# Two graph layers over an edge list: 432 tiles of one bucket each become 332 pure and 50 mixed tiles, and the second layer moves into the loop's block

## The reference

```python
def layer0(h, edges, W, b):            # 41,250 edges (src, tgt), 1,250 nodes, 512 features
    x_ij = concatenate([h[src], h[tgt]], axis=1)        # 41,250 x 1,024
    m_ij = relu(x_ij @ W.T + b)                         # W: 512 x 1,024
    return segment_sum(m_ij, src, 1250)

def layer1(h, src, dst, edge_weight, W, alpha):
    g = h @ W.T
    out = segment_sum(g[src] * edge_weight[:, None], dst, 1250)
    return where(out >= 0, out, alpha * out)

h = maximum(layernorm(x), 0);  x = x + layer0(h, ...)
h = maximum(layernorm(x), 0);  x = x + layer1(h, ...)
```

## Time and profile before

| | us |
|---|---|
| median of 3 runs (lowest, highest) | 1081.85 (1081.13, 1082.65) |
| profiled execution | 1083.92 |
| its span | 1082.2 |
| first placing column starts (DVE) | 40.78 |
| first edge product starts | 287.18 |
| last edge product starts | 951.92 |
| W1's load is issued | 961.23 |
| first second-layer product starts | 971.90 |

### The profile page before, as it was taken

The page is one execution under the profiler, slowest core; times in us unless marked ns, Lnnn a source line. Parts: engine busy times, 40 slices in busy tenths (PEclk is TensorE's granted clock), DMA queues, the critical chain, the costliest instruction groups (busy, mean ns, idle before and its releaser), DMA issues. The chain is left out here.

```text
span 1082.2 us, 22605 instructions
## 1 busy us (share of the span) xinstructions
PE 1023.7 (95%) x4879; PEld 814.1 (75%) x4880; DVE 949.4 (88%) x1801; ACT 836.0 (77%) x1769; POOL 716.6 (66%) x1042
## 2 busy tenths in 40 slices
PE   5698999999799999999999999999999999959997
PEld 4386887777588788777888777777778877748775
DVE  7798899888599999999999999999999999973454
ACT  6777798788688888888888888888888888844210
POOL 3888787867567777777777777777777777730000
PEclk9999999999899999999999999999999999979999
DMA  7000000000111111111111111111111111010011
GB/s 209 2 2 3 2 3 2 4 2 2 54 44 43 42 43 39 43 41 41 44 38 43 42 43 43 38 43 42 42 43 38 43 42 42 25 39 1 20 34 42
DMA packets 37249, 38.15 MB, mean 35 GB/s; under 512 B 5990, under 2 KB 33431, under 8 KB 37212
## 3 DMA queue, kind: packets, MB, share of 16 engines
q1 hardware_dynamic: 32512, 37.07, 11.0%
q0 software_dynamic: 4416, 0.30, 1.6%
q10 hardware_dynamic: 284, 0.33, 0.1%
HBM read 34.04 MB, written 3.36 MB: 35 GB/s over the span
## 5 line engine op out<-in xcount | busy, mean ns | idle before, releaser
L1076 ACT ACTIVATE msg_hi<-edge_ps 128x512 fp32r<-128x512 f32 x432 | 257.8, 597 | 81.7 <-PE edge_ps L1000 81.7
L930 POOL TENSOR_TENSOR M<-M,pair_w 125x125 f32 x432 | 210.9, 488 | 162.0 <-DVE pair_w L1134 122.5
L1148 DVE SCALAR_TENSOR_TENSOR msg_lo<-edge_ps,msg_hi 128x512 fp32r<-128x512 f32 x432 | 290.8, 683 | 20.7 <-ACT msg_hi L1076 15.1
L374 POOL DMA_INDIRECT edge_table<-fields,row_no x136 | 176.7, 1299 | 50.3 <-issue 40.5
L914 POOL TENSOR_TENSOR hot_w<-hot_d,weight_l 128x252 fp32r<-128x252 bf16 x216 | 180.8, 837 | 0.0
L737 ACT ACTIVATE lane_piece<-hot_lane,fields 125x128 fp32r<-125x128 bf16 x498 | 155.6, 391 | 30.6 <-DVE hot_lane L455 30.2
L955 PE MATMUL node_ps<-msg_hi,hot_s 128*125 128x512 f32 x432 | 176.5, 409 | 0.2 <-DVE msg_lo L1148 0.2
L994 PE MATMUL edge_ps<-b_hi,turned_d 125*128 x432 | 172.8, 400 | 1.3 <-ACT turned_d L1060 0.7
L624 PE MATMUL psum<-hot_tile,lane_piece 125*128 125x432 f32 x582 | 157.2, 394 | 16.5 <-ACT lane_piece L737 16.3
L999 PE MATMUL edge_ps<-a_hi,turned_s 125*128 x432 | 171.4, 397 | 0.1
L995 PE MATMUL edge_ps<-b_lo,turned_d 125*128 x432 | 171.3, 397 | 0.0
(11 more groups left out here) (206 smaller groups left out, 1726.6 us busy)
## 6 DMA issues: line engine op xcount, KB each, us to landing
spread<-edge_rows SPq DMA_DIRECT2D x214, 125.0 KB
out_dram<-result SPq DMA_DIRECT2D x10, 250.0 KB
edge_table<-fields,row_no POOLq DMA_INDIRECT x136, 2.6
w_in<-in_L_gnn_W_dram SPq DMA_DIRECT2D x1, 2048.0 KB, 11.6
S<-in_x_dram SPq DMA_DIRECT2D x1, 1792.0 KB
w_in<-in_L_gnn_W_dram SPq DMA_DIRECT2D x1, 1024.0 KB, 5.2
S<-in_x_dram SPq DMA_DIRECT2D x1, 448.0 KB
edge_table<-zeros SPq DMA_DIRECT2D x1, 432.0 KB, 15.3
```

What stands on the lines that cost most here:

```text
L374: pool.indirect_dma_start(table_dram[:, :], bass.IndirectOffsetOnAxis(ap=row_no[:, c:c + 1], axis=0), fields[:, c, 0:TABLE_FIELDS], None). ...
L930: pool.tensor_tensor(part, part, pair_w[h][:, j, 0, 0:BN], ALU.add).then_inc(m_added, 1)
L1076: act.activation(msg_hi[j][:], edge_ps[j][:], ACT.Relu).then_inc(hi_ready, 1)
L1148: dve.scalar_tensor_tensor(out=msg_lo[j][:], in0=edge_ps[j][:], scalar=0.0, in1=msg_hi[j][:].bitcast(F32), op0=ALU.max, op1=ALU.subtract). ...
```

## The change

Each bucket used to fill up its last tile alone. Now the buckets of a source block and two neighbouring destination blocks (2p, 2p+1) share one mixed tile. The 50 mixed tiles come first in the tables (52 columns, 13 groups, MIXC = 52) and last in time; the other edges lie in 332 pure tiles (83 groups), which run as before. NT goes from 432 to 384.

- Slots: the tile counts of a bucket pair are rounded so that the rest of both goes to the pair's mixed tile; a third row beside base_hi and base_lo (`base_up`) moves the odd bucket's slots by multiples of 65536 when they pass its pure tiles. `slots` decodes this with 12 instead of 5 steps. An edge's code has a sign for "odd destination block"; decoding gives local_d (negative for odd in mixed tiles) and local_o = -local_d, so that a one-hot of either is empty for the other's edges.
- Counts: the counting products for chunk k+2 stand seven columns before the end of chunk k, and ACT's copy one column before it.
- A mixed tile has six edge products: two for the even, two for the odd destination block (third one-hot `turned_o`, one buffer), two for the source block; addresses are constants. Its weights product is two products of 252 columns (both destination blocks side by side) that sum high and low in PSUM. Odd tiles' weights are copied by ACT and added to M by POOL in one addition of 250 columns, even ones' are added by DVE directly from PSUM.
- node_ps is summed over the five mixed tiles of a source block and added to S once; then DVE makes the block's statistics, beside the following tiles.
- The second layer's programs follow in the same block, without the barrier between blocks. W1's load is issued once the last edge product is through. Each result is stored as 112 and 13 rows.
- hot_d and hot_s are made from a 16-bit iota (`iota_h`), hot_d has room for two destination blocks, `square` is bf16.

```diff
+NBP = NBLK // 2
+NMIX = NBLK * NBP
+MGRP = -(-NMIX // GRP)
+MIXC = MGRP * GRP
+NGRP = -(-(E // TILE + NBLK * (PAIR - 1)) // GRP)
+PURE = NGRP * GRP
+NT = MIXC + PURE
+COUNT_BACK, COPY_BACK = 7, 1
...
                     def slots(k):
+                        quotient, upper, whole, after = (planes[:, i, :] for i in range(4))
+                        tile, at = tile_no[:, k % 2, :], lane[:, k % 2, :]
+                        own(dve.tensor_reduce(slot[:], planes.rearrange("p b c -> p c b"), AX.X, ALU.add))
+                        own(dve.tensor_scalar(quotient, slot[:], -MID_SLOT, 1.0 / UPPER, ALU.add, ALU.mult))
+                        own(dve.tensor_scalar(upper, quotient, MAGIC, -MAGIC, ALU.add, ALU.add))
...
+                            part = i - last + COUNT_BACK
+                            if k + 2 < NCHUNK and 0 <= part < 3:
+                                count(k + 2, range(CHUNK // 3 * part, CHUNK // 3 * (part + 1)))
...
+                            if k + 2 < NCHUNK and i == FIRST[k + 1] - FIRST[k] - 1 - COPY_BACK:
+                                copy_counts(k + 2)
...
+                def weigh_mixed(m):                                       # POOL
+                    u, j = divmod(m, GRP)
+                    h = m % 2
+                    if j == 0:
+                        pool.wait_ge(hots_d, NGRP + u + 1)
+                    if m < 2:
+                        pool.wait_ge(m_ready, NGRP * 2 + h - 1)
+                    else:
+                        pool.wait_ge(mix_ps, m - 1)
+                    for f, part in enumerate((weight_h[:].bitcast(F32), weight_l)):
+                        pool.tensor_tensor(hot_w[h][:, f], hot_d[(NGRP + u) % 2][:, :, j, :],
+                                           part[:, m:m + 1].unsqueeze(2).to_broadcast([P, 2, OHW]), ALU.mult).then_inc(mix_weighed, 1)
+                def add_mixed(m):
+                    pool.wait_ge(mix_copied, (m + 1) // 2)
+                    blocks = M[:, 2 * m:2 * m + 2, :]
+                    pool.tensor_tensor(blocks, blocks, pair_w[1][:, 0, :, 0:BN], ALU.add).then_inc(mix_pooled, 1)
+                for m in range(2, NMIX):
+                    weigh_mixed(m)
+                    if m % 2 == 1 and m > GRP:
+                        add_mixed(m - GRP)
...
+                def edges_mixed(m):                                       # PE
+                    if j == 0:
+                        pe.wait_ge(turned, n + 1)
+                    pe.matmul(ps, turned_d[k][:, at], b_hi[:, first], start=True, stop=False)
+                    pe.matmul(ps, turned_d[k][:, at], b_lo[:, first], start=False, stop=False)
...
+                    if j == 0:
+                        pe.wait_ge(turned, n + 3)
+                    pe.matmul(ps, turned_o[:, at], b_hi[:, second], start=False, stop=False)
+                    pe.matmul(ps, turned_o[:, at], b_lo[:, second], start=False, stop=True).then_inc(edge_ready, 1)
...
+                for m in range(NMIX):
+                    edges_mixed(m)
+                    if m < 2:
+                        sum_tile(NGRP - 1, PAIR + m, (NGRP - 1) % 2)
+                    else:
+                        sum_mixed(m - 2)
+                    if m in (1, 3):
+                        weights(NGRP - 1, (NGRP - 1) % 2, m // 2)
+                    if m >= GRP:
+                        weights_mixed(m - GRP)
...
+                def next_mixed(v, j):                                     # ACT
+                    made = (turned_d[g % 2], turned_s[g % 2], turned_o)
+                    if j > 0:
+                        one_hot_of(n + j, made[j - 1])
+                    if j < 3:
+                        act.wait_ge(turned, n + j)
...
+                        act.activation(square[:], spread[pair + f][:], ACT.Square, bias=minus_no[0:BN, :],
+                                       scale=-1.0 if j == 2 else 1.0).then_inc(squared, 1)
+                def copy_mixed(m):
+                    act.wait_ge(mix_ps, m + 1)
...
+                        act.wait_ge(mix_pooled, m // 2)
+                    act.copy(pair_w[1][:, 0], m_ps[1][:, 0]).then_inc(mix_copied, 1)
...
+                sp.wait_ge(edge_ready, PURE + NMIX)
+                sp.dma_start(w1_in[:], w1.rearrange("(o p) i -> p o i", p=P)).then_inc(w1_loaded, 16)
+                for b in range(NBLK):
+                    sp.wait_ge(out_ready, b + 1)
+                    for rows in SPLIT:
+                        sp.dma_start(out[b * BN:(b + 1) * BN, :][rows], result[b % 2][rows]).then_inc(stored[b % 2], 16)
```

More of the change, by code:

```diff
@@ L101, in build @@
         ident = sb("ident", [P, P], F32)
-        iota = sb("iota", [P, NT], F32)
+        iota_h = sb("iota_h", [P, P], F16)
         ident_b = sb("ident_b", [P, P], BF16)
@@ L1034, in _ @@
                 turn(0, second=True)
[L1035 removed]
+                with pe.Fori(1, TURNS) as it:
                     turn(it)
[L1037 to L1044 removed]
+                at = offsets(REST)
@@ L1424, in build @@
+        tail.close()
         scope_m.close()
```

766 lines of the change are left out of this document (473 added, 293 removed).

## The result

| | before | after |
|---|---|---|
| median of 4 runs each, same chip (us) | 1082.25 (1081.13 to 1084.27) | 1026.09 (1022.98 to 1027.34) |
| profiled execution, its span | 1083.92, 1082.2 | 1027.34, 1025.4 |
| first placing column starts | 40.78 | 48.50 |
| last placing column starts | 274.6 | 278.5 |
| first edge product starts | 287.18 | 290.91 |

The ratio is 0.9475, 95% interval 0.9448 to 0.9502: faster by 5.0 to 5.5%. 1021 was forecast, 1009 to 1037 the range.

The account below looks back on a forecast made before the run. PE was taken to pace the edge loop, with DVE 3% behind. Loop start 284.2, pure tiles 511.5, mixed 108.1, hole 8.4 and second layer 109.0 sum to a span of 1021.2 us; forecast 1021, range 1009 to 1037.

Parts of the forecast that it names:

- the 3 for hand-overs: Mixed tiles: late turned_o and the change from pure to mixed tiles cost 3 us, bounds 0 and 10.
- held by 0.18: Mixed groups: the next turned_o is ready 2.85 us after the tile's start, PE needs it at 3.03.
- Rivals 1 and 4: Mixed tiles: 1, POOL paces them, +29, 1050, chance 0.15; 4, PE waits for turned_o every group, 1106, chance 0.02.
- Rival 2: First part: added steps are paid, stalls only move to another wait; +11.7 instead of -3, 1036, chance 0.13.
- rival 3: First part gains all it can, hand-overs cost nothing: -7 and -3, 1011, chance 0.10.
- the load leads: Hole before the second layer: W1's load, first transposes and copies set its length, 8.4 us, bounds 7.5 and 12.
- The chain that I called sooner: Hole: last sum, block addition, two weights tiles behind DVE's M additions, done at 5.8 us, ahead of W1's load.
- (a): Before the first column: added steps for tile counts, slot bases, base_up and edge codes cost 3.9 us.
- (b): First part, slots: seven more steps cost 1.3 us before the first column and 5.2 in the four others.
- (c): First part: hot_tile and placing products shrink from 432 to 384 columns, saving DVE 4.9 us.
- (d): First part: earlier counts and copies remove 7.3 us of DVE's count stalls and 3.3 of its placing-product waits.
- a third of the second: First part: of DVE's 9.9 us of waits for placing products, 3.3 go.

Follow-up runs that it names:

- all_by_gpsimd: Changed kernel with the weights of all 50 mixed tiles copied by ScalarE and added into M by GpSimd; median 1029.38 us, ratio to before 0.9532.
- pool_idle_at_code: Changed kernel with GpSimd's weight copies and later work held until VectorE has made the edge codes; median 1022.80 us, ratio to before 0.9466.
- after_again: The changed kernel run once more without any edit; median 1031.25 us, ratio to before 0.9518.
- before_counts_moved: Kernel before with only the counting products and ScalarE's copy of the counts moved earlier; median 1080.18 against 1085.21 us, ratio 0.9954.
- one_zero_product: Changed kernel with one added product of zeros in the first part's columns without products of A or B; median 1027.68 us, ratio to before 0.9467.
- w1_early: Changed kernel with W1's tile placed over A's first four blocks, its load issued some 12 us earlier; median 1029.69 us, ratio to before 0.9515.

## Why the prediction was right, and where it was not

**Pure and mixed tiles (right, for the reason given).** TensorE paces both. 332 tiles took 509.8 (508.6 to 510.4 in twelve profiles) against 511.5; 50 mixed tiles 107.5 start to start against 105.1 + 3. Of the 3 for hand-overs 2.4 came, all at the change from pure to mixed: 0.8 for turned_o and 1.4 for a first weighing. The wait for turned_o that held by 0.18 held in all 12 groups. The waits of TensorE from 800 to 909 us:

```profile
PE m_ps L1265 <- POOL hot_w L1112: 1.4, 1, 1.4
PE edge_ps L1242 <- ACT turned_o L1356: 0.8, 1, 0.8
```

**The rivals.** Rivals 1 and 4 were wrong. GpSimd had more in hand than 1.0 (all_by_gpsimd), and no stall of turned_o came back in later groups. Rival 2 came in part, see the first part; rival 3 didn't.

**The hole (size nearly right, cause wrong).** "Afterwards the load leads": it doesn't. The chain that I called sooner, of additions, weights and copies, leads. Its length was right: the last four weights products start 5.74 after the last edge product is through (914.23 and 908.49; the same in pool_idle_at_code), where I had 5.8; they waited for VectorE's addition of tile 46 into M at 913.67, behind the copy of h2. What I left out is what stands behind it in TensorE's queue: these products (0.86) and all 16 transposes of W1, not the first four (1.91 and a wait of 0.18 for VectorE's copy in pool_idle_at_code). That makes 8.7. The remaining 1.1 between 8.9 and 10 (start to start) is the clock during the transposes. So the 8.4, against 9.60 in after and 8.7 in after_again counted alike, was near by luck: its terms are those of another chain.

**Second layer (the store right, half of the gain not foreseen).** 1.5 for the store instead of 1.3; the other 1.5 of the 3.0 is the clock of G's first products, which I had not counted. Kernel before, then after, the first 6 us of the second layer:

```profile
971.90:978.00 6.10, 6.10 (x22) 4.85 (x23) 1.07 (x4) 2.98 (x5) 0.00 (x0) 0.72 0.01 3
```
```profile
918.09:924.00 5.91, 5.91 (x28) 4.81 (x27) 2.66 (x4) 3.90 (x7) 0.00 (x0) 0.94 0.01 3
```

**The first part (the step that failed).** Edit (a) had 3.9 plus 1.3 and measured 7.7. The price of a code step, 0.5, was right for one alone. The error is in the cover: the neighbours in the trace of before (0.79 and 0.97 for two such steps at 25.49 and 26.31, against 0.50 and 0.47 alone) already ran beside GpSimd, and the two added ones fell into GpSimd's conversions too, where all four took 1.24 to 1.45. From the first of these steps to the predicated copies it was 1.64 us before and is 5.51 now: 3.9 more where 1.1 was taken, the whole excess of (a). The two steps in the kernel before:

```profile
25.49 0.79 DVE L534 SCALAR_TENSOR_TENSOR local<-local 125x330 f32<-125x330 f32 x1
26.31 0.97 DVE L536 TENSOR_SCALAR fields<-local 125x330 int32<-125x330 f32 x1
```

I had weighed that same rule of contention for the mixed tiles, where it didn't matter, and not here, where it did.

Edits (b) and (c) were right on VectorE: its busy time between first and last column rose by 0.8 (205.28 to 206.04), where 5.2 and 4.9 leave 0.3; hot_tile's mean went from 496 to 470 ns, 26 less where 25 was taken. In (d) the counts' stalls went as forecast (10.9 to 3.1), but "a third of the second", 3.3 us of waits for placing products, did not come: they grew by 4.3. This 7.6 covers the column part's whole error of 6.5 (-10.3 forecast, 233.8 to 230.0 measured).

So the two terms that failed are the 1.1 for the code steps in (a) and the "third of the second" in (d). The loop starts 3.7 later than before, where the forecast had 3 earlier and rival 2 had 11.7 later. Rival 2 came in part: stalls moved to another wait, though to the one for placing products and not to row_no (9.8, 9.7 before).

Two things stand in the place of the term in (d). One is TensorE at half its clock in one to three stretches a run: 6.5 of the 14.2 us of waits stand within 10 us of the two stretches (at 97.6, 99.7, 101.8 and at 194.8, 198.1, 199.6), and two stretches by the estimate cost 4. The other is the moved counting products themselves, which stand ahead of placing products: before_counts_moved shows 2.1 us of such waits at full clock, and one_zero_product, without any low clock behind 72 us, still waited 10.4, not 6.6. The waits at 97.6 to 101.8 have both causes beside them, so the shares in the changed kernel aren't separated. Why the clock falls where it does stays open, as does why the one profile of before has no such stretch behind 62 us while that of before with its counts moved has one. Decoding took 0.2 less instead of 1.3 more.

## What to carry to other kernels

Price an added step by a neighbour only after looking at what ran beside that neighbour: 0.50 alone was 1.45 beside GpSimd, and a step's place decides between them. A stall that is removed by moving work earlier in another engine's queue can come back in part as a wait behind that work. An engine's margin is read from its busy time, not from a sum of durations; full GpSimd (98%) cost nothing. Where TensorE isn't the bound, don't count on the waits for it shrinking with its work, and look for its granted clock in every stretch before comparing single profiles.

## What had not been expected of the hardware

- The granted clock in the rows can miss a slow stretch: in the profile of before 41 to 61 us are shown at 1.00, but twelve placing products of 432 columns took 4.37 us there (0.364 each) against 0.213 each in the earlier trace rows; in before_counts_moved the same twelve took 3.87 us, and there the record shows 0.50 up to 59.6 us. The pitch of products of known width is the better witness.
- The low-clock stretches of one program aren't the same in every profile: from 89 and 192 us in after, 154 and 236 in after_again, 191 and 232 in w1_early, whose first part is that of after. Seven of the eight profiles with the same columns have one that starts between 187 and 194, so their place isn't random. With them varies the start of the loop, 287.9 to 295.1. The second half of the same program repeats within 0.2 us in the mixed tiles.
